# Two-layer attention and expert kernel on one core: the early expert blocks of the second layer are cut from five batches' rows instead of six (21 blocks instead of 24), with their buffer rings moved and ten planner allowances in place of five

## What is computed

```
layer 0:  h = layernorm(x)*(1+ca)+sa;  x += ga * causal_attention(h)      # 16 heads of 128, 4 key/value heads
          h = layernorm(x)*(1+cb)+sb;  x += gb * (shared(h) + top2 of 8 experts(h))    # hidden 176
layer 1:  h = layernorm(x)*(1+ca)+sa;  x += ga * linear_attention(h)      # one head of 128, sigma = elu+1
          h = layernorm(x)*(1+cb)+sb;  t = rmsnorm(h)*norm_w
          G = softmax over the top 4 of 16 router logits of t
          x += gb * (h + sum_e G[e] * (act(t @ w1[e] + b1[e]) @ w2[e] + b2[e]))   # hidden 256
```

## Time and profile before

| | us |
|---|---|
| median of 3 timed runs | 1075.15 (1074.07 to 1079.61) |
| the profiled execution, its own time | 1071.31 |
| its span, first to last instruction | 1069.5 |
| PE busy in the span | 986.5 (92%) |
| DVE busy | 716.1 (67%) |
| ACT busy | 675.1 (63%) |
| POOL busy | 427.9 (40%) |
| mean granted TensorE clock | 0.961 of full speed |

### The profile page before, as it was taken

The page is one execution under the profiler, slowest core; times in us unless marked ns, Lnnn a source line. Parts: engine busy times, 40 slices in busy tenths (PEclk is TensorE's granted clock), DMA queues, the critical chain, the costliest instruction groups (busy, mean ns, idle before and its releaser), DMA issues.

```text
span 1069.5 us, 20514 instructions
## 1 busy us (share of the span) xinstructions
PE 986.5 (92%) x6020; PEld 828.6 (77%) x6020; DVE 716.1 (67%) x2545; ACT 675.1 (63%) x1944; POOL 427.9 (40%) x450
## 2 busy tenths in 40 slices
PE   7999999999999999999999989977897689999990
PEld 4679888878888887877887868855686579999880
DVE  2554656775767866775885686675877557887780
ACT  2657677676776875876677567743635356776660
POOL 3322422344424432362245136113164654665663
PEclk9999999999999999999999989977989899999995
DMA  9929982998895100020011023235175797999864
GB/s 309 304 63 329 376 321 77 375 375 309 291 378 186 61 21 1 32 82 20 1 62 51 21 79 112 99 149 191 26 198 129 201 224 198 229 224 223 206 140 79
DMA packets 93726, 180.54 MB, mean 169 GB/s; under 512 B 9949, under 2 KB 29085, under 8 KB 92717
## 3 DMA queue, kind: packets, MB, share of 16 engines
q1 hardware_dynamic: 73467, 148.55, 42.0%
q0 software_dynamic: 18800, 30.30, 12.5%
q10 hardware_dynamic: 1346, 0.36, 0.1%
HBM read 77.71 MB, written 107.99 MB: 174 GB/s over the span
## 4 chain that ended last, share of the span: by engine, by line
PE 78%; DVE 8%; DMA 5%; issue 3%; ACT 2%; DVEq 1%; POOL 1%; another core or an unknown queue 1%; ACTq 0%; POOLq 0%; SPq 0%
PE bank L1033 10%; PE bank L1005 10%; PE bank L1069 9%; PE bank L1023 5%; PE bank L995 5%; PE bank L1078 4%; DMA accD<-BC,to 4%; PE bank L984 4%; PE bank L861 3%; PE bank L994 3%; PE bank L955 3%; PE bank L1024 3%; PE bank L870 3%; PE bank L1014 2%; PE bank L939 2%
## 5 line engine op out<-in xcount | busy, mean ns | idle before, releaser
L1069 PE MATMUL bank<-RB 128*128 128x128 f32 x1264 | 158.3, 280 | 8.7 <-ACT RB L1341 3.2
L1069 PEld LDWEIGHTS bank<-RB 128*128 128x128 f32 x1264 | 151.6, 196 | 12.8 <-issue 6.2
L1863 POOL TENSOR_TENSOR RB<-RB 128x512 f32<-128x512 f32 x64 | 67.1, 1049 | 222.6 <-DVE RB L1643 219.8
L1033 PE MATMUL bank<-RA,RB 128*128 128x256 f32 x512 | 132.4, 381 | 1.4 <-ACT RB L1235 1.4
L1334 ACT ACTIVATE RB<-RA,nw 128x512 f32 x158 | 105.3, 714 | 36.7 <-issue 17.6
L1005 PE MATMUL bank<-RA 128*128 128x256 f32 x512 | 122.3, 382 | 0.0
L1005 PEld LDWEIGHTS bank<-RA 128*128 128x128 f32 x512 | 95.6, 192 | 13.2 <-issue 1.0
L1033 PEld LDWEIGHTS bank<-RA,RB 128*128 128x128 f32 x512 | 91.3, 190 | 12.9 <-ACT RB L1235 1.7
L1078 PE MATMUL bank<-RB,BC 128*128 128x256 f32 x316 | 85.3, 396 | 12.8 <-DVE BC L1770 12.7
L1839 POOL TENSOR_TENSOR qs<-qs,half 128x4 f32<-128x4 f32 x64 | 66.0, 1031 | 76.3 <-DVE qs L1652 65.0
L1918 POOL DMA_INDIRECT out<-BC,to x40 | 64.3, 1608 | 62.3 <-DVE BC L1777 17.8
(11 more groups left out here) (260 smaller groups left out, 2418.2 us busy)
## 6 DMA issues: line engine op xcount, KB each, us to landing
xsD<-BC SPq DMA_DIRECT2D x17, 4232.0 KB, 31.0
RB<-in_w2b SPq DMA_DIRECT2D x79, 256.0 KB
RB<-xsD SPq DMA_DIRECT2D x55, 264.5 KB
BC<-modD SPq DMA_DIRECT2D x16, 512.0 KB, 4.1
X<-xsD SPq DMA_DIRECT2D x24, 264.5 KB
RA<-in_w SPq DMA_DIRECT2D x2, 2048.0 KB, 7.2
RA<-in_w SPq DMA_DIRECT2D x6, 512.0 KB, 8.1
RA<-in_L_attn_Wq SPq DMA_DIRECT2D x1, 2048.0 KB, 13.9
```

What stands on the lines that cost most here:

```text
L1033: m = pe.matmul(bank[5][:, t * 256:t * 256 + 256], OT[:, u % 2, t * 128:t * 128 + 128], Wo[:, h, :], start=(h == 0 and t == 0), stop=(h == ...
L1069: m = pe.matmul(ps[:, 128 * j:128 * j + 128], WS[:, n % 2, c, 128 * j:128 * j + 128], XT[:, n % 2, c * 128:c * 128 + 128], start=(c == 0), ...
L1863: pool.tensor_tensor(sq, qrow, qrow, ALU.mult).then_inc(mine("q_sq", p), 1)
```

## The change

`FIRST, PART` become 21, 5: the first table is made after batch 4's router, and the first 21 blocks read rows of batches 0 to 4 only; 58 blocks are left for the loop. The ring of five row buffers lay in `X[:, 0:12]`, which belongs to six batches; now four places are in the rows of `X` of the first five batches and the fifth lies where the attention keeps `qrow`, so that `xb(4)` waits for the last query work. `YB` grows from three to five places, and `to` from four to six. The scratch of `spread` moves out of the buffers that attention still uses, and its waits go. `e_a` gets two waits (on `s_x(5, 1)` and `f_add(0, 5)`). The planner's allowances become ten, and four weights of POOL rise.

```diff
-FIRST, PART = 24, 6
+FIRST, PART = 21, 5
-        "POOL": "y_add 1.6 tok .3 ... f_gain 1.1 f_x 1.15 f_send 1.2",
+        "POOL": "y_add 1.87 tok .8 ... f_gain 1.5 f_x 1.2 f_send 1.3",
-    KV, LATE, EARLY, UNIT, FILL = 0.0, 0.0, 0.1, 0.1, .3
+    KV, QUERY, FIRSTS, SHARED, DENSE, LINEAR, LATE, UNIT, FILL, TURN = 0.04, 0, 0.1, 0.02, 0.0, 0.06, 0.1, 0.1, 0.19, -0.09
-            p.chain(EARLY, ffn0(b))
+            p.chain(FIRSTS, ffn0(b))
-            p.chain(KV, shared(b, i))
+            p.chain(SHARED, shared(b, i))
-                p.chain(EARLY, dense(b, i, r))
+                p.chain(DENSE, dense(b, i, r))
-                p.chain(EARLY, turned(b, i, h))
+                p.chain(DENSE, turned(b, i, h))
-            p.chain(LATE, lin_attn(b))
+            p.chain(LINEAR, lin_attn(b))
-        bk = yield do("n_mm", part, first=True, after=[("s_x", PART - 1, 1)] + ...
+        bk = yield do("n_mm", part, first=True, after=...
-        after = [("n_bi", 0), ("store", PART - 1), ("f_send", 1, PART - 1, 1, 3)] + ...
+        after = [("n_bi", 0), ("store", PART - 1), ("f_send", 1, PART - 1, 1, 3)] + [("q_t", NU // 2 - 1)] * (n == RINGS[0] - 1) + ...
-        yield do("x_t", n, bank=1, first=True, late=0, after=[("x_out", n - 1)] * (n > 0))
-        yield do("x_out", n, bank=1, last=True, late=0, ...
+        yield do("x_t", n, bank=1, first=True, late=TURN, after=[("x_out", n - 1)] * (n > 0) + [("h_mm", n - 2)] * (n >= 2))
+        yield do("x_out", n, bank=1, last=True, late=TURN, ...
-        yield do("y_out", n, ..., after=[("y_add", n - 3)] * (n >= 3))
+        yield do("y_out", n, ..., after=[("y_add", n - 5)] * (n >= 5))
-        yield do("tok", n, after=[("xb", n)] + [("y_add", n - 4)] * (n >= 4))
+        yield do("tok", n, after=[("xb", n)] + [("y_add", n - 6)] * (n >= 6))
-    p.chain(EARLY, mod_rows(0))
-    p.chain(KV, queries())
+    p.chain(FIRSTS, mod_rows(0))
+    p.chain(QUERY, queries())
...
+        YB = [free[:, 1280 + 256 * i:1536 + 256 * i] for i in range(3)] + [RB[:, 5120:5376], X[:, 0:2 * PART, :].rearrange(...)[:, 2304:2560]]
+        XB = ([X[:, 0:2 * PART, :].rearrange(...)[:, 530 * i:530 * i + 530] for i in range(4)] + [RC[:, 4944:5474]],
+              [RC[:, 530 * i:530 * i + 530] for i in range(RINGS[1])])
@@ xb(n), n < FIRST
+                    if n == RINGS[0] - 1:
+                        on.wait_ge(*done("q_t", NU // 2 - 1))
+                        on.wait_ge(*done("q_sq", NU // 2 - 1))
@@ xb(n), n >= FIRST
+                    if n - FIRST in (9, 10):
+                        on.wait_ge(*done("y_out", FIRST - 1))
+                        on.wait_ge(*done("tok", FIRST - 1))
@@ e_a(n)
+                on.wait_ge(*done("s_x", NB - 3, 1))
+                on.wait_ge(*done("f_add", 0, NB - 3))
@@ y_out(n)
+                on.wait_ge(*done("res", 0, NB - 1))
-                    on.wait_ge(*done("y_add", n - 3))
+                    on.wait_ge(*done("y_add", n - 5))
```

More of the change, by code:

```diff
@@ L410, in spread @@
     def spread(part):
-        bk = yield do("n_mm", part, first=True, after=[("s_x", PART - 1, 1)] + [("f_t", 1, NB - 1), ("f_gate", 1, NB - 1)] * part)
+        bk = yield do("n_mm", part, first=True, after=[("f_t", 1, NB - 1), ("f_gate", 1, NB - 1)] * part)
         yield do("n_blk", part, bank=bk)
@@ L424, in block @@
     def block(n):
-        after = [("n_bi", 0), ("store", PART - 1), ("f_send", 1, PART - 1, 1, 3)] + [("y_out", n - RINGS[0]), ("tok", n - RINGS[0])] * (n >= RINGS[0])
+        after = [("n_bi", 0), ("store", PART - 1), ("f_send", 1, PART - 1, 1, 3)] + [("q_t", NU // 2 - 1)] * (n == RINGS[0] - 1) + [("y_out", n - RINGS[0]), ("tok", n - RINGS[0])] * (n >= RINGS[0])
         yield do("xb", n, slot=n % RINGS[0], by=16, after=after)
@@ L430, in block @@
         p.chain(FILL, token(n))
-        yield do("x_t", n, bank=1, first=True, late=0, after=[("x_out", n - 1)] * (n > 0))
-        yield do("x_out", n, bank=1, last=True, late=0, after=[("h_mm", n - 2)] * (n >= 2))
+        yield do("x_t", n, bank=1, first=True, late=TURN, after=[("x_out", n - 1)] * (n > 0) + [("h_mm", n - 2)] * (n >= 2))
+        yield do("x_out", n, bank=1, last=True, late=TURN, after=[("h_mm", n - 2)] * (n >= 2))
         yield do("h_mm", n, bank=2 + n % 2, first=True, after=[("w_in", n)] + [("h_mm", n - 1)] * (n > 0))
-        yield do("e_a", n, bank=2 + n % 2, after=[("res", 0, NB - 1)] * (n == 0) + [("e_act", n - 2)] * (n >= 2) + [("e_b", n - 1)] * (n > 0))
+        yield do("e_a", n, bank=2 + n % 2, after=[("res", 0, NB - 1), ("s_x", NB - 3, 1)] * (n == 0) + [("e_act", n - 2)] * (n >= 2) + [("e_b", n - 1)] * (n > 0))
         p.chain(FILL, clamp(n))
@@ L439, in block @@
         yield do("y_mm", n, bank=4 + n % 2, first=True, after=[("w2x", n)] + [("y_mm", n - 1)] * (n > 0))
-        yield do("y_out", n, bank=4 + n % 2, last=True, after=[("y_add", n - 3)] * (n >= 3))
+        yield do("y_out", n, bank=4 + n % 2, last=True, after=[("y_add", n - 5)] * (n >= 5))
         yield do("y_add", n, slot=n % 2, by=16, after=[("tok", n)] + [("y_add", n - 2)] * (n >= 2))
     def token(n):
-        yield do("tok", n, after=[("xb", n)] + [("y_add", n - 4)] * (n >= 4))
+        yield do("tok", n, after=[("xb", n)] + [("y_add", n - 6)] * (n >= 6))
     def clamp(n):
@@ L579, in build @@
         AC = free[:, 0:512].rearrange("p (r n) -> p r n", r=2)
-        AB, YB = (free[:, 512 + 768 * i:1280 + 768 * i].rearrange("p (r n) -> p r n", r=3) for i in range(2))
+        AB = free[:, 512:1280].rearrange("p (r n) -> p r n", r=3)
         wmod = [BC[:, 3 * l:3 * l + 3, :].rearrange("p b n -> p (b n)").rearrange("p (c n) -> p c n", c=2) for l in range(2)]
-        XB = (X[:, 0:12, :].rearrange("p t n -> p (t n)")[:, 0:530 * RINGS[0]].rearrange("p (r n) -> p r n", r=RINGS[0]),
-              RC[:, 0:530 * RINGS[1]].rearrange("p (r n) -> p r n", r=RINGS[1]))
+        YB = [free[:, 1280 + 256 * i:1536 + 256 * i] for i in range(3)] + [RB[:, 5120:5376], X[:, 0:2 * PART, :].rearrange("p t n -> p (t n)")[:, 2304:2560]]
+        XB = ([X[:, 0:2 * PART, :].rearrange("p t n -> p (t n)")[:, 530 * i:530 * i + 530] for i in range(4)] + [RC[:, 4944:5474]],
+              [RC[:, 530 * i:530 * i + 530] for i in range(RINGS[1])])
         F0, LA, F1 = 0, 5108, 7798
@@ L596, in build @@
         dactT = sc(F0 + 4064, 704).bitcast(BF16).rearrange("p (c n) -> p c n", c=11)
-        nw_ = free[:, 0:400], sc(F1, 400)
+        nw_ = sc(F0 + 4768, 328), sc(F1, 328)
         h1, s1T, xnL = pair(sc(LA, 512)), pair(sc(LA + 1024, 512)), pair(sc(LA + 2178, 512))
@@ L671, in rows @@
             part = n >= FIRST
-            return XB[part][:, (n - FIRST * part) % RINGS[part], :]
+            return XB[part][(n - FIRST * part) % RINGS[part]]
         def table(i, n):
@@ L1725, in n_tab @@
                 on.wait_ge(ch.sem, ch.n)
[L1726 removed]
+                dve.tensor_tensor(w[0:E, 168:248], w[0:E, 8:88], w[0:E, 88:168], ALU.subtract).then_inc(mine("n_tab", part), 1)
             def n_bi(part):
@@ L1905, in tok @@
                 on.wait_ge(*done("xb", n))
-                if n >= 4:
-                    on.wait_ge(*done("y_add", n - 4))
-                pool.tensor_copy(to[:, n % 4:n % 4 + 1], rows(n)[:, 256:257].bitcast(U32)).then_inc(mine("tok", n), 1)
+                if n >= 6:
+                    on.wait_ge(*done("y_add", n - 6))
+                pool.tensor_copy(to[:, n % 6:n % 6 + 1], rows(n)[:, 256:257].bitcast(U32)).then_inc(mine("tok", n), 1)
             def y_add(n):
```

25 lines of the change are left out of this document (11 added, 14 removed), and 2 rows, old and new, of the table ENGINE.

## The result

The changed kernel takes 1043.75 us (median, 1042.61 to 1046.54, 4 runs) and the kernel before, beside it, 1077.34 us (1074.07 to 1079.61, 4 runs): ratio 0.9694, 95% interval 0.9657 to 0.9732. Repeated in a later group it stood at 0.9727 (0.9694 to 0.9759). The kernel before had medians from 1069.6 to 1077.3 us over the groups of this study, so kernels of different groups are compared by ratio, not by time. The forecast was a gain of 17.4 us, to 1057.8. The medians of this group are 33.6 us apart; the profiled execution, 1043.59 us with a span of 1041.7 against 1071.31 and 1069.5, gained 27.7 and 27.8.

A forecast was written before the change was run, and what follows sets the result against it. PE was taken as the bound, with a thin part from 716 to 880.6 us. The loop opening 26.0 us earlier, less 8.6 us for three more loop blocks, gave 17.4 us: 1075.15 to 1057.8 us, range 1045 to 1073.

The forecast's parts named there:

- Term 5: Allowances reorder all chains: 0 before 704 us, bounds -8 and +8; in the thin part counted inside the 0.76.
- the 0.76: Packing of PE work where chain and blocks run together, 747 to 840 us, taken for the stretch before the loop.
- The hole: Before 704 us, at 620 to 640: 8.0 us of PE lost; it may close or another may open.
- Term 2: Loop opening: 105.0 us of PE work at 0.76 take 138.2 us, so it opens at 854.6, 26.0 us earlier.
- rival B: Thin part before the loop: packing no better than 0.69, opening at 868.6, gain 3.4 us, 1071.8 us; chance 0.13.
- Term 1: First early block: its h_mm starts at 716.4 us, bounds 715 and 722, 30.6 us earlier, held by w1.
- Term 3: Loop: 58 instead of 55 blocks, each 2.88 us of a full PE, +8.6 us that nothing hides.
- Term 4: Left-over blocks before the loop: longer rings shrink or remove waits before y_mm, 8.9 us, not added to the sum.
- The signs: From first h_mm to end: start near 716, clock above 0.85, last send 835 to 848, opening 849 to 862.
- A: Thin part: early blocks raise the clock, the chain shortens; opening 843 to 849, gain 23 to 29 us; chance 0.15.
- C: Where PE is full: the new order opens holes, 8.0 us each; slower from the third, 1081.8 us; chance 0.09.
- D: Early blocks still start near 747 us; only longer rings (8.9) and fewer blocks (8.6) count, 1066.3 us; chance 0.08.

The follow-up runs named there:

- e7_dense: The changed kernel with one allowance set back, DENSE 0.1 instead of 0.0 (the dense experts'); ratio 0.9860 to the kernel before.
- p3_early09: The kernel before with one allowance changed, EARLY 0.09 instead of 0.10; ratio 0.9900 to the unaltered kernel before.
- c_after: The changed kernel itself, unaltered, timed and profiled once more; ratio 0.9727 to the kernel before, median 1042.74 us.
- r3_wait_only: The changed kernel in its own order, but each y_out waits for the y_add three blocks back instead of five; ratio 0.9778 to the kernel before.
- e1_parts: The changed kernel (21 blocks from five batches, rings, waits) with all allowances and POOL weights as before; ratio 0.9928 to the kernel before.
- e2_allow: The kernel before (24 blocks from six batches, old rings) with the ten allowances and new POOL weights; ratio 0.9907 to the unaltered kernel before.
- p4_kv01: The kernel before with one allowance changed, KV 0.01 instead of 0.00; ratio 1.0061 to the unaltered kernel before.

## Why the prediction missed, step by step

The time, 1043.75, lay below the range's low end of 1045 and 14 us below the forecast.

**Term 5 is the step that failed.** It gave the allowances "0, bounds -8 and +8" for the part before 704 and "inside the 0.76" for the thin part. Two things happened. The hole closed, the better bound, -8.0. And 15.3 us of the chain's work moved from the tail into the dense part: +15.3 there, and 15.3/0.627 = 24.4 us of tail less, net -9.1. Together 17 of the 27.8 us. (Over the whole part before attention's end the loss fell by 6.3 us, so smaller gaps took back some of the 8.0.) I had seen the allowances as tie-breaks among chains inside the tail, and not asked which chains lie across the border between a full stretch and a thin one. `DENSE` falls below `UNIT` by 0.1, so the dense experts stop yielding to the attention units of later batches; `e7_dense` shows that this alone moves the work, and `p3_early09` that 0.01 does half of it. The work moved is measured; that it is worth 9.1 us is worked out from the rate, and no pair of runs shows that size apart from the orders' spread.

**Term 2, the packing: the amount of chain was wrong, and hardly the rate.** "At 0.76, 105.0 us take 138.2". From the first `h_mm` to the opening it took 115.4. Busy time times mean granted clock, where clock and busy share vary within a stretch, counts too much: over 704 to 881, 139.69 x 0.86 = 120 against 110.7 counted by shape. But it did so in the work and in the rate alike. By shape, the chain from 716 to 880.6 was 35.0 us and not 44.5, and the stretch 747 to 840 ran at 0.70 and not 0.76; (60.5 + 35.0)/0.70 is 136 us, nearly the same. The changed kernel has 82.5 us of work there, at 0.716. Its chain is 22.0 us in place of 35.0, which is 19 of the 23 us missing; the rate is 3 of them. Before, 19.0 us of chain ran between attention's end and the first `h_mm`, and now 4.0; behind the first `h_mm` it was 21.5 and is 22.0. So the work that moved is the work that filled the 42.8 us before the first block, and this is term 5 again.

Over the whole tail, before was at 0.627 and the changed kernel at 0.657 (86.8/132.1); 86.8 us at the two rates differ by 6.3 us. What makes it denser stays open; the granted clock of the tail rose from 0.86 to 0.90 with it. With the parts alone, the loop opened at 868.8, where rival B had it (868.6): its gain of 7.7 us is nearer to B's 3.4 than to the forecast's 17.4.

**Term 1, the first block.** The first `h_mm` came at 729.4, not 716.4, outside the bounds 715 to 722. 8.5 us are the later end of attention. The other 4.5 are w1's landing: 8.9 to 12.9 us after issue in the rows above (7.3 to 9.8 in the kernel before), issued 712.77 to 714.83, and ACT's `w_in` waited for it at 728.03. They are inside the 6 us that I had as a bound for `w2x` in the way, which is issued from 716.62; whether it was `w2x` or other traffic isn't shown. The first `xb` went out at 693.35 and not near 668, because batch 4's store did, at 688; w1 hid that. The late start cost little, since 18 of the 21 blocks were begun by the last send all the same.

**Term 3 came out in the sum**: opening to end +8.1 for a forecast of +8.6 (196.9 for 197.5). From the opening to the last block's first product a block takes 2.87 us (163.5/57), where before it took 2.92 (157.7/54), so this part grew by 5.8; the end grew by 2.3 (33.4 for 31.1). That the two make 8.1 is in part luck: in `c_after` they are 165.3 and 37.0, 202.3 in all. **Term 4** was right to add nothing: there is no wait over 3 us before a `y_mm` at the changeover (the longest is 0.84), but `r3_wait_only` has none either (2.57), so the ring is not what removed it.

**Sum by mechanism**: hole -8.0; moved chain -9.1; three blocks, +8.6 in the loop and 8.6/0.627 = 13.7 off the tail, -5.1; rate -6.3. That is -28.5 for -27.8 measured. The split between the last two and the moved chain is accounting and not experiment.

**The signs.** Of the eight that were to show it right, two came true: opening to end 196.9, and no long wait before a `y_mm`. The first `h_mm` came at 729.4, the clock of 716 to 747 was 0.83 and not above 0.85, 18 blocks and not 19 were begun by the last send, the send came at 830.3 and not after 835, the loop's first `xb` 7.7 us behind it and not 6, and the opening at 844.8 and not after 849.

**The rivals.** A had the opening (843 to 849) right and the reason wrong. The clock went from 0.86 to 0.90 over the tail, but the last send came 10 us earlier because work of the chain had gone from in front of it: it ends 136.0 us after attention in the kernel before, and 140.5 and 145.5 in `e1_parts` and `e7_dense`, where the blocks start early and the chain has not moved; it is 117.6 in the changed kernel and 123.4 in `e2_allow`, where it has. B holds for the parts alone. C had the mechanism right, orders that open and close holes of 8 us, and the sign wrong here; `p4_kv01` is the slower kernel that it described. D is out: the blocks did start earlier.

What stays open is how the last 1% divides among the ring's re-planning, `PART` and the weights; a single order of each can't tell.

## What to carry to other kernels

Where a full stretch is followed by a thin one, look first for work in the thin one that could stand in the full one: it costs its own length there and, at the rates of this case, saves 1.5 to 1.6 times that here, and a change in priority alone can move it. Fill a chain's gaps only up to what is used up by the chain's end (18 of 21 blocks here; six of 24 were left over). And where one engine order is planned by tie-breaks, time the neighbours of an order (here up to 1% away at a change of 0.01, and 1.6% apart over six) before a part is given credit for 1%.

## What the hardware showed beside

An addition on DVE with both inputs in SBUF takes 0.42 us at 128x256, but 1.01 and 1.57 us where a 512-wide POOL operation lies beside it (timeline, after):

```profile
716.68 0.43 DVE L1688 TENSOR_TENSOR SC<-bank,BC 128x256 f32<-128x256 f32 x1 [0.71 <-remote]
716.76 1.10 POOL L1884 TENSOR_TENSOR SC<-SC,BC 128x512 f32<-128x512 f32 x1
717.14 1.01 DVE L1690 TENSOR_TENSOR X<-X,SC 128x256 f32<-128x256 f32 x1
...
718.08 0.41 DVE L1688 TENSOR_TENSOR SC<-bank,BC 128x256 f32<-128x256 f32 x1
718.52 1.57 DVE L1690 TENSOR_TENSOR X<-X,SC 128x256 f32<-128x256 f32 x1
718.73 1.08 POOL L1889 TENSOR_TENSOR X<-X,SC 128x512 f32<-128x512 f32 x1
```

In both, DVE's ends 0.3 us after POOL's (718.15 and 717.86, 720.09 and 719.81), while the operation at 716.68, with one input in PSUM, keeps 0.43 beside the first POOL operation. (The one at 718.08 lies between the two and says nothing.) The Trainium skill, "SBUF — State Buffer" (Who interferes with whom), says that DVE and GpSimd share one port pair under an exclusive lock, which a DVE operation with two SBUF inputs needs too; these rows agree. Beside POOL operations of 128x4, though, it isn't seen: at 568.32 such an addition takes 0.42 us beside a POOL `qs` operation of 1.00 us from 567.48. I hadn't priced this when POOL's `f_gain` and `f_x` were set among DVE's `s_x`.
